# Zeros by a transfer, column sums by VectorE and one fp32 matmul: two small pieces of preparation in a two-layer kernel

## What is computed

```python
x = x + _L0_ffn_ref(_L0_cond_ref(x, cond, ...), L0_ffn_weight)      # grouped conv 9 taps, then int8 matmul 1024x1024
x = x + _L1_ffn_ref(_L1_cond_ref(x, cond, ...), W, b, A, Bmat, LiMEs)
```

```python
agg_b = att @ bias_k
out = jnp.einsum('boi,bih->boh', agg_w, x) + agg_b[:, :, None]       # input of the ffn
...
H = jnp.einsum('btd,od->bto', x, W) + b
z = jnp.einsum('btd,dr->btr', x, A)                                  # rank 32
H_slice = H[:, anchors, :E]                                          # 8 logits, every second token
delta_slice = jnp.einsum('bar,er->bae', z[:, anchors], LiMEs)
```

## Time and profile before

| what | us |
|---|---|
| median of 3 runs | 615.25 |
| lowest, highest | 614.13, 617.0 |
| the profiled execution, its own time | 615.68 |
| its span in the trace | 613.9 |
| TensorE busy | 598.1 (97%) |
| VectorE busy | 432.7 (70%) |
| ScalarE busy | 357.8 (58%) |
| GpSimd busy | 375.1 (61%) |

### The profile page before, as it was taken

One profiled execution on the slowest core, in us unless ns is written; L12 is line 12 of the kernel. 1 busy time (PEld: TensorE's weight loads), 2 busy tenths in 40 slices (PEclk: granted clock), 3 DMA queues, 4 the chain that ended last, 5 costly groups with the idle time before them and its releaser, 6 DMA issues.

```text
span 613.9 us, 16142 instructions
## 1 busy us (share of the span) xinstructions
PE 598.1 (97%) x6455; PEld 341.7 (56%) x6488; DVE 432.7 (70%) x881; ACT 357.8 (58%) x622; POOL 375.1 (61%) x252
## 2 busy tenths in 40 slices
PE   8999999999999999999999999999999999999997
PEld 4656666667777777666554444444444444444443
DVE  6978998988999999986887757754635444335535
ACT  5879998889999999876635244453233333133000
POOL 3336545546776766654888945989787655875200
PEclk9999999999999999999999999999999999999999
DMA  8978987878899999684183025765446443545203
GB/s 335 357 255 298 371 314 261 290 269 316 311 327 328 329 318 324 230 305 140 56 303 125 34 70 202 282 233 190 160 171 207 133 172 140 171 138 171 87 17 137
DMA packets 38344, 136.24 MB, mean 222 GB/s; under 512 B 5004, under 2 KB 5292, under 8 KB 38225
## 3 DMA queue, kind: packets, MB, share of 16 engines
q1 hardware_dynamic: 33518, 118.43, 54.9%
q10 hardware_dynamic: 4752, 16.78, 6.9%
HBM read 87.95 MB, written 47.24 MB: 220 GB/s over the span
## 4 chain that ended last, share of the span: by engine, by line
PE 84%; DVE 3%; issue 2%; ACT 0%; DVEq 0%
PE ps L908 41%; PE ps L611 14%; PE ps L516 8%; PE ps L708 7%; PE ps L595 4%; PE ps L890 2%; PE ps L580 2%; PE ps L656 2%; PE ps L651 1%; DVE yb L1451 1%; PE ps L620 0%; PE ps L624 0%; PE ps L691 0%; DVE w_part L1527 0%; PE ps L676 0%
## 5 line engine op out<-in xcount | busy, mean ns | idle before, releaser
L611 PE MATMUL ps<-wqT,yq_both 128*128 128x512 bf16 x479 | 115.2, 378 | 5.8 <-issue 4.5
L1276 POOL TENSOR_TENSOR x<-x_in,f_all 128x512 f32<-128x512 f32 x64 | 74.4, 1163 | 49.7 <-DVE f_all L1488 49.6
L1280 POOL TENSOR_TENSOR x_split<-x_ph,x_split 128x1032 f16<-128x1032 f32 x25 | 53.7, 2148 | 55.2 <-ACT x_split L989 55.2
L1016 ACT ACTIVATE yv<-yb,yinv 128x128 f32<-128x128 f32 x256 | 77.9, 388 | 0.4 <-DVE yinv L1479 0.4
L1315 POOL TENSOR_TENSOR ring<-ring 128x512 f32<-128x512 f32 x56 | 72.9, 1301 | 4.3
L611 PEld LDWEIGHTS ps<-wqT,yq_both 128*128 128x128 bf16 x512 | 45.5, 99 | 46.2 <-issue 0.8
L1488 DVE SCALAR_TENSOR_TENSOR f_all<-ps,tok_scale,wsc_b 128x512 f16<-128x512 f32 x64 | 47.9, 749 | 18.9 <-PE ps L611 18.1
L516 PE MATMUL ps<-x_split,conv_h 128*64 128x256 f16 (+1 forms) x1248 | 60.1, 274 | 0.1
L516 PEld LDWEIGHTS ps<-x_split,conv_h 128*64 128x64 f16 (+1 forms) x1248 | 47.5, 108 | 9.9 <-issue 7.9
L1059 ACT ACTIVATE ring<-ring,pair_inv 128x1024 f32<-128x1024 f32 x28 | 30.6, 1139 | 36.0 <-DVE wst L1793 11.8
L1806 DVE SCALAR_TENSOR_TENSOR x_in<-ps,unscale,x_in 128x512 f32<-128x512 f32 x30 | 22.5, 750 | 40.8 <-PE ps L908 40.7
(11 more groups left out here) (349 smaller groups left out, 1294.3 us busy)
## 6 DMA issues: line engine op xcount, KB each, us to landing
x_in<-in_x SPq DMA_DIRECT2D x32, 512.0 KB, 6.1
x_scratch<-x SPq DMA_DIRECT2D x32, 512.0 KB, 3.6
x_ph<-in_x_phases SPq DMA_DIRECT2D x31, 516.0 KB, 5.1
x_scratch<-ring SPq DMA_DIRECT2D x26, 512.0 KB, 5.4
ring<-x_scratch SPq DMA_DIRECT2D x26, 512.0 KB, 5.3
x_in<-x_scratch SPq DMA_DIRECT2D x12, 512.0 KB, 3.9
out<-x_in ACTq DMA_DIRECT2D x12, 512.0 KB, 3.3
wst<-in_w_rows SPq DMA_DIRECT2D x10, 512.0 KB, 6.7
```

The source lines that it names most:

```text
L611: last = mm(acc_bank(t, h), yqT[:, t % 2, p, :], wqT[:, p, h * HALF:(h + 1) * HALF], start=p == 0, stop=p == PH - 1)
L1016: last = A(yv[:, s, :], yb[:, t % 2, s, :], ACT.Copy, scale=yinv[:, s:s + 1], bias=MAGIC)
L1276: g.tensor_tensor(x1[:, t % 2, s], x_in[:, t % 3, s], f16[:, s], ALU.add).then_inc(sem("x1_ready"), 1)
L1280: g.tensor_tensor(x_split[:, (t - SPLIT) % 2, 1, :], phases(t), x_split[:, (t - SPLIT) % 2, 0, :], ALU.subtract).then_inc(sem("xl_ready"), 1)
```

## The change

The zeros of rows 32 to 63 of zT come by a transfer on SyncE's queue. Its source is chanmax_rep, a 128 by 128 tile that VectorE sets to zero in the first microseconds and of which only rows 0 to 7 are written later; rows 32 to 63 of it, 512 bytes each, are repeated 32 times. The transfer stands behind bias_b and ahead of the wait for agg_b. ScalarE's instruction is gone. The column sums are taken in two steps: VectorE adds the 8 blocks of z_f into z_sum (128 by 40) at the start of its step 5, and TensorE does one fp32 matmul of z_sum against a column of fp32 ones.

```diff
-        ones16 = sb("ones16", [P, 1], F16)
+        ones = sb("ones", [P, 1], F32)
+        z_sum = sb("z_sum", [P, ZR], F32)
...
             sp.dma_start(bias_b[:, :], b_ffn[0:E].rearrange("(a l) -> a l", a=1).to_broadcast([P, E])).then_inc(sem("b_loaded"), 16)
+            sp.wait_ge(sem("s_max_zeroed"), 2)
+            zeros = chanmax_rep[R:64, :, :].rearrange("p a c -> p (a c)").unsqueeze(1).to_broadcast([64 - R, NTOK // P, P])
+            sp.dma_start(zT[R:64, :].rearrange("p (t n) -> p t n", n=P), zeros).then_inc(sem("zeros_ready"), 16)
             sp.wait_ge(sem("agg_b_ready"), 1)
...
             def z_bias_sums():
-                pe.wait_ge(sem("z_w_ready"), 1)
-                for n, c in ((0, 0), (1, 64)):
-                    for k in range(NL):
-                        last = mm(bank(7)[64:ZW, 0:1], z_w[:, k, c:c + ZR], ones16[:, 0:1],
-                                  start=n == 0 and k == 0, stop=n == 1 and k == NL - 1)
-                last.then_inc(sem("z_col_psum"), 1)
+                pe.wait_ge(sem("z_w_ready"), 2)
+                pe.wait_ge(sem("ones_ready"), 2)
+                mm(bank(7)[64:ZW, 0:1], z_sum[:, :], ones[:, 0:1], start=True, stop=True).then_inc(sem("z_col_psum"), 1)
...
             A(att_e[:, :], att[:, :], ACT.Exp, bias=att_s[:, 0:1]).then_inc(sem("att_exp_ready"), 1)
-            act.wait_ge(sem("zeros_ready"), 1)
-            A(zT[R:64, :].rearrange("p (a e) -> p a e", e=2)[:, :, 1], z_w[R:64, 0, 0:1].to_broadcast([64 - R, NTOK // 2]), ACT.Copy).then_inc(sem("zeros_ready"), 1)
             wq_out(0)
...
-            g.memset(ones16[:, :], 1.0)
+            g.memset(ones[:, :], 1.0).then_inc(sem("ones_ready"), 1)
...
                     if t == 0:
-                        dve.wait_ge(sem("zeros_ready"), 2)
+                        dve.wait_ge(sem("zeros_ready"), 17)
...
                     scale_phases(c + LEAD - 1)
+                if c == 5:
+                    dve.wait_ge(sem("rank_hi_ready"), 4)
+                    v.tensor_reduce(z_sum[:, :], z_f[:, :, :].rearrange("p k r -> p r k"), AX.X, ALU.add).then_inc(sem("z_w_ready"), 1)
                 if c >= 6 and c % 2 == 0:
```

## The result

| | kernel before | changed kernel |
|---|---|---|
| median of 11 runs each, one chip, us | 615.25 | 618.62 |
| lowest, highest | 614.13, 617.0 | 616.9, 620.69 |
| ratio of the times, 95% interval | | 1.0041 [1.0027, 1.0056] |
| the profiled execution, its span | 615.68, 613.9 | 618.63, 616.8 |

The change costs 0.4%, 2.5 us by the ratio, within the half per cent that I had named as no change, but with an interval that leaves 1 out. The forecast was +0.4 us. By the ratio the time is 617.8, just under the upper end of the range; the two medians are 3.4 apart, and 618.62 is 0.6 above that end.

The account below looks back on a forecast made before the run. TensorE is busy 97%, but between 48 and 69 us ScalarE was taken to set the end. Zeros 0, matmul 0, VectorE's sum 0 and transfer +0.4 us moved the median from 615.25 to 615.7; range 614.0 to 618.0.

Parts of the forecast that it names:

- ScalarE's zeros: Removing ScalarE's 2.09 us instruction at 9.13 us only lengthens its following wait for TensorE's transposes; gain 0.
- One fp32 matmul: On TensorE at 55.37 us, one matmul of 0.2 us replaces sixteen taking 0.48; saves about 0.3, worth 0 off the chain.
- VectorE's sum: Block sum added at 54.90 us, 0.5 us (1.0 if strides double it), fits a 0.60 us gap; cost 0.
- T: Delay of SyncE's queue behind the new transfer, from agg_b's save on: 2.2 us, between 1.3 and 3.2.
- Slack of 1.5 for tile 7's phases: Phases landing at 45.3 us may land at 46.8 free; up to 0.9 of shift absorbed; ScalarE late 0 to 0.7, taken +0.4.
- From ScalarE's delay to the end: Between 48 and 69 us ScalarE sets the end, so whatever makes it later there makes the kernel later.
- The sum: All terms together, 0 + 0 + 0 + 0.4 = +0.4 us, median 615.7; chance of this forecast 0.49.
- All hidden: Rival: the queue delay is at most 1.5 us or slack takes it; 615.25, within 0.2; chance 0.30.
- A gain: Rival: ScalarE does not hold TensorE at 68.63 us, so 0.3 us of saved issue stays; 614.9; chance 0.07.
- Slow pieces: Rival: 1024 pieces of 512 bytes halve the transfer rate, queue delay 6.4 us, time 620.2; decides from 4.6; chance 0.07.
- The sum on VectorE is slow: Rival: VectorE's block sum takes over 1 us for strided input; +0.4 to +0.8, 615.9; chance 0.04.
- The signs named: Expected in the new profile: agg_b about 34.6, tile 7's phases 46.6 to 47.5, ScalarE 0 to 1 us later, z_sum about 54.9.

Follow-up runs that it names:

- early_weights: sums_only with ScalarE's two writes of z_f and one of conv_h moved from step 4 to step 3; 1.0028 against the kernel before.
- sums_only: Kernel before with only the new column sums (z_sum on VectorE, one fp32 matmul), ScalarE's zeros kept; ratio 1.0037.
- sums_again: The same kernel as sums_only, timed once more against the kernel before; ratio 1.0027.
- sums_moved: sums_only with z_sum later on VectorE and the fp32 matmul behind step 5's integer product; 1.0044 against the kernel before.
- after: The changed kernel, whole change, first comparison with the kernel before; median 618.62 us, ratio 1.0041.
- after_again: The whole changed kernel, timed once more against the kernel before; ratio 1.0019.
- zeros_only: Kernel before with only the zeros by transfer and ScalarE's instruction gone, sixteen fp16 matmuls kept; ratio 1.0013.
- load_32rows: Kernel before plus a transfer at the new one's place: 512 KB from memory in 32 rows of 16 KB, ScalarE's zeros kept; ratio 1.0019.
- half_transfer: Kernel before plus half the new transfer (16 repeats of 512 bytes into the same 32 rows), ScalarE's zeros kept; ratio 1.0000.
- sums_padded: sums_only with 14 one-column matmuls into an unread column ahead of the fp32 one; 0.9994 against the kernel before.

## Why the prediction was right or wrong, step by step

- **ScalarE's zeros, gain 0.** Right. ScalarE has 2.2 us less work, and z_bias(0) came no earlier, counted from conv(4), in any kernel without the instruction.
- **One fp32 matmul, 0.2 us, saves 0.3 of issue, worth 0.** It takes 0.24 by its record, and the mixing follows 0.16 us behind its start, where 0.48 were before: 0.3 saved, as said. That it is worth 0 in the stretch holds too: conv(4) to max_rows is 24.27 to 24.29 in all sums kernels but early_weights. But 0 for the whole edit was wrong: sums_only is at 1.0037 and sums_again at 1.0027, about 0.3%, and the price is in no wait of this stretch.
- **VectorE's sum, 0.5 us, between bounds of 0.5 and 1.0.** 0.77: the middle of the two, and I had taken the lower end for a stride that no row showed. TensorE waits 0.17 to 0.20 us, not 0 to 0.1. Harmless, as sums_moved shows.
- **T = 2.2, bounds 1.3 and 3.2.** This is the term of the sum that was mis-sized. It was 3.9 in after, above the bound, and 2.6 in after_again and 2.4 in zeros_only, inside it and above the middle. I had split few rows (my upper bound) from small pieces (a rival that doubled it); the runs show 1.5 and 1.1 for each alone and 2.4 to 3.9 for both together. The estimate of 2.7 by the rule of the Trainium skill ("SBUF — State Buffer", "Door 1: The DMA port swizzle") on rows 32 to 63 was nearer than the middle that I took, but load_32rows, which fills the same rows at 1.5, does not fit it.
- **Slack of 1.5 for tile 7's phases, up to 0.9 of the shift absorbed.** The place and the slack were right: 4.1 us of later landing became 2.41 on ScalarE (and conv(4) was 0.17 later), and half_transfer, 1.3 later, cost nothing. The absorption failed in after and after_again, where the landing moved by 4.1 and 2.8, more than T; in zeros_only it moved by 1.5 for a T of 2.4, and 0.7 of that because the phases were issued later, at 40.5. The execution decides, not the program alone.
- **From ScalarE's delay to the end, one to one.** Right: 2.41, 2.40 and 2.41 us at the phases' high half, z_bias(0) and max_rows.
- **The sum.** +0.4 predicted, +2.5 measured in the first comparison, +1.2 in the second (1.0019). The mechanism named was the one at work in both profiles, with +2.24 and +1.18 in the stretch, and the sign was right; the size was not. Missing was a term for the sums, which cost about 0.3% by sums_only and sums_again, for a reason that stays open. I had asked only who waits for whom, and no row of the kernel before prices anything else. That the time by the ratio still lies within the range is partly luck: its upper end was T at 3.2 with the scatter of a median, and no part of it stood for the sums.
- **The rivals.** *All hidden* holds for the transfer in zeros_only and half_transfer, not in after. *A gain* fell: sums_only has the shorter issue and is slower. *Slow pieces* named pieces and rows together, as the runs show, but T stayed below the 4.6 at which it was to decide. *The sum on VectorE is slow*: 0.77, no.
- **The signs named.** agg_b about 34.6 (36.28), tile 7's phases 46.6 to 47.5 (49.4), ScalarE 0 to 1 late (2.8), each outside in the direction of a larger T (agg_b came at 34.99 in after_again and 34.75 in zeros_only, close to the forecast); z_sum at 54.9 was 56.80, because ScalarE's delay had already reached TensorE (the wait of 1.22) and VectorE.

The parts do not add up in the ratios: transfer alone 1.0013, sums alone 1.0037 and 1.0027, both 1.0041 and 1.0019. The intervals are too wide to say how much of after's loss is which part; only for the profiled execution is it the transfer, by its rows.

No version beat the kernel before. sums_padded equals it.

## What to carry to other kernels

A transfer ahead of others in one queue costs its time minus the smallest slack of what stands behind it; find that slack from landing times and first readers, and take the delay at the upper end or above when both few rows and small pieces come together. An edit that is free by every wait can still cost some tenths of a per cent when the busiest engine is busy for 97%; pad its instruction count back and time that before explaining the loss by the edit's own work. One profile is one execution: here two of the same kernel differed by a microsecond in the very wait that was to be explained.

## What the hardware showed that I had not expected

- 512 KB more in the queue: 1.1 us of delay in 512-byte pieces within SBUF over 128 rows, 2.4 to 3.9 in the same pieces over 32 rows, 1.5 in long pieces from memory into 32 rows; 179 to 185 GB/s with every DMA engine taken.
- The issue of the small save of agg_b held SyncE for 2.87 to 4.11 us in the four profiles with a transfer of 1024 pieces ahead of it, and for 0.51 or 0.52 in all others, that of half_transfer with 512 pieces included.
- VectorE's fp32 rescaling of 0.75 us took 2.49 beside a GpSimd instruction of 2.13 us.
- TensorE's pauses of 0.2 to 1.5 us without a releaser stand only behind its records number 705 plus multiples of 256; which of these places get one, and how long it is, differs from execution to execution.
